# Second attention of a gated cross-attention block: the slot's projection on TensorE moved ahead of the transposes

## What is computed

```
x = x + tanh(g_xattn[0]) * attention0(layernorm(x), ctx)
x = x + tanh(g_ffn[0])   * quantised_feed_forward(layernorm(x))
x = x + tanh(g_xattn[1]) * attention1(layernorm(x), ctx, mask)
x = x + tanh(g_ffn[1])   * mixture_of_experts(layernorm(x))
```

```
q, k, v = x @ wq + bq, ctx @ wk + bk, ctx @ wv + bv      (per head)
score = q k^T / 4 * mask; where it is 0: -1e9
heads = softmax(score) v ;  out = heads @ wo + bo
```

## Time and profile before

| | |
|---|---|
| median of 3 runs | 1631.07 us (1628.36 to 1631.3) |
| the profiled execution's own time | 1624.04 us |
| its span in the trace | 1622.2 us |
| PE busy in the span | 1399.8 us (86%) |
| DVE busy | 1230.6 us (76%) |
| ACT busy | 1103.1 us (68%) |
| mean granted PE clock | 0.936 of full speed |

### The profile page before, as it was taken

One profiled execution on the slowest core, in us unless ns is written; L12 is line 12 of the kernel. 1 busy time (PEld: TensorE's weight loads), 2 busy tenths in 40 slices (PEclk: granted clock), 3 DMA queues, 4 the chain that ended last, 5 costly groups with the idle time before them and its releaser, 6 DMA issues. The chain is left out here.

```text
span 1622.2 us, 40480 instructions
## 1 busy us (share of the span) xinstructions
PE 1399.8 (86%) x15436; PEld 995.7 (61%) x15436; DVE 1230.6 (76%) x3108; ACT 1103.1 (68%) x2440; POOL 179.3 (11%) x177
## 2 busy tenths in 40 slices
PE   5899999999999993492379898989898689999996
PEld 3577666666667662340366666666666367788884
DVE  5888888888888877758778999898898877344443
ACT  5777777777777763467428889888888654366663
POOL 1000001100000002200000000000000100034443
PEclk9999999999999997797688999999999889999998
DMA  6122232332322211000011121211010072122221
GB/s 206 46 86 85 85 107 90 96 107 85 98 93 91 76 60 59 0 1 26 0 57 50 54 77 54 77 51 28 18 35 12 21 251 68 56 35 46 49 45 23
DMA packets 64924, 105.67 MB, mean 65 GB/s; under 512 B 7449, under 2 KB 38914, under 8 KB 63586
## 3 DMA queue, kind: packets, MB, share of 16 engines
q1 hardware_dynamic: 58018, 94.83, 18.6%
q0 software_dynamic: 6720, 8.27, 3.2%
HBM read 68.88 MB, written 35.11 MB: 64 GB/s over the span
## 5 line engine op out<-in xcount | busy, mean ns | idle before, releaser
L1482 ACT ACTIVATE a_p<-a_s,a_nb 112x375 f32<-112x375 f32 x256 | 140.9, 598 | 26.5 <-DVE a_nb L1585 26.2
L271 PE MATMUL a_ps_o<-a_vh,a_pt 125*128 125x64 f16 (+1 forms) x1536 | 152.8, 183 | 2.6 <-ACT a_pt L1495 0.8
L1402 PE MATMUL a_ps_t<-ident,a_p 112*128 112x112 f32 x768 | 118.1, 284 | 42.6 <-ACT a_p L1482 41.3
L273 PE MATMUL a_ps_o<-a_vh,a_pt 125*128 125x64 f16 (+1 forms) x1536 | 151.1, 182 | 0.0
L272 PE MATMUL a_ps_o<-a_vl,a_pt 125*128 125x64 f16 (+1 forms) x1536 | 151.0, 182 | 0.0
L618 ACT ACTIVATE a_p<-a_ps_s,a_nb 112x375 f32<-112x375 f32 x256 | 144.0, 573 | 2.7 <-DVE a_scaled L768 2.1
L271 PEld LDWEIGHTS a_ps_o<-a_vh,a_pt 125*128 125x128 f16 x1536 | 133.5, 98 | 14.7 <-ACT a_pt L1495 6.4
L626 ACT ACTIVATE a_pt<-a_ps_t 125x336 f16<-125x336 f32 x256 | 101.5, 448 | 59.4 <-PE a_ps_t L555 59.1
L1402 PEld LDWEIGHTS a_ps_t<-ident,a_p 112*128 112x128 f32 x768 | 79.6, 146 | 97.8 <-issue 82.7
L272 PEld LDWEIGHTS a_ps_o<-a_vl,a_pt 125*128 125x128 f16 x1536 | 130.8, 98 | 11.0 <-issue 0.2
L1585 DVE CUSTOM_DVE_ANT_0 a_s<-a_s,a_fill 112x375 f32<-112x375 f32 x256 | 130.3, 547 | 5.5
(11 more groups left out here) (443 smaller groups left out, 4486.7 us busy)
## 6 DMA issues: line engine op xcount, KB each, us to landing
a_piece<-in_w SPq DMA_DIRECT2D x72, 256.0 KB, 3.0
split_weights<-a_pair SPq DMA_DIRECT2D x72, 256.0 KB, 3.3
w<-split_weights SPq DMA_DIRECT2D x8, 1024.0 KB, 6.1
a_ctx<-in_ctxT SPq DMA_DIRECT2D x16, 375.0 KB, 3.6
ctx<-a_cx SPq DMA_DIRECT2D x16, 375.0 KB, 4.2
a_cx<-ctx SPq DMA_DIRECT2D x16, 375.0 KB, 5.9
w1h<-split_weights SPq DMA_DIRECT2D x2, 1792.0 KB, 14.8
w1l<-split_weights SPq DMA_DIRECT2D x2, 1792.0 KB, 18.0
```

The lines of the kernel that those rows point to most:

```text
L271: nc.tensor.matmul(out, wh, mh, start=(i == 0), stop=False)
L273: last = nc.tensor.matmul(out, wl, mh, start=False, stop=(i == n - 1))
L1402: mm = nc.tensor.matmul(ps_t[:, 2 * (g % 2) + i, t * S:(t + 1) * S], p32[:, g % 2, i, t * KV:t * KV + 128], ident32[0:S, 0:S], start=(t == ...
L1482: nc.scalar.activation(p32[:, g % 2, i, 0:NC], s2[:, g % 2, i, :], ACT.Exp, bias=nb[:, g % 2, i:i + 1], scale=-1.0).then_inc(exp_done, 1)
```

## The change

Within each slot of PE's loop, the slot's jobs are issued directly behind the scores, and the transposes of the pair ahead directly behind the jobs. The order of all other steps, and the order on the other engines, is as before.

```diff
@@ -1434,10 +1434,10 @@
             for g in range(SLOTS):
                 if g < G:
                     scores(g)
+                for name, b in slot_job(g):
+                    job(name, b)
                 if 0 <= g - 1 < G:
                     transposes(g - 1)
-                for name, b in slot_job(g):
-                    job(name, b)
                 if 0 <= g - 2 < G:
                     weighted_values(g - 2)
                 if 0 <= g - 1 < G:
```

## The result

The changed kernel takes 1732.89 us (median of 4 runs, 1730.77 to 1735.23), the kernel before 1629.71 beside it: ratio 1.0649, 95% interval 1.0614 to 1.0683 (the two medians divided give 1.063, inside it). That is slower by 103 us, where 1695 was forecast (64 slower) with a range up to 1730. The sign was right, the size was not, and the time lies outside the range.

A forecast was written before the change was run, and what follows sets the result against it. No engine is full; a ring of handovers bounds the second attention's pair loop. Profiled execution 1624.04 plus 60 (structure) plus 4 (clock) gives 1688; the median lies 7.0 above, so 1695 us, range 1665 to 1730.

The forecast's parts named there:

- The structural term: Second attention's pair loop: uncovered tail and job waits lengthen a batch by 4.21 or 3.64 us, 60 us in sum.
- my 3 for batch 0: Estimated growth of batch 0, which starts at half clock and lacks OT and W: 3 us.
- The tail: Slot's end, transposes' start to next scores: with no job between, ACT's copy can't be hidden; 2.07 us per slot.
- both rings: PE's pass waiting for ACT's copy (tail 2.07 us), and each job waiting for the previous job's low half.
- the wait for the low half: Slot's head: a job starts 0.83 us after its scores, not 0.58, where the previous job used both engines.
- The clock term: More PE idle in the stage means somewhat more time at half clock: +4 us, bounds 0 to +14.
- I take +4, near the first: Clock cost in the stage, near the bound of no more half-clock stretches (0): 4 us.
- twice as many stretches: Upper bound of the clock cost: the stage's later 37 us of half clock doubled, +14 us.
- The prediction's own sign of being wrong: Slots 1 and 6 still near 3.1 us, the pass not waiting, or the stage's mean clock under 0.85.
- the third rival: PE's half clock is no longer lifted for long stretches of the stage: 1765 to 1840 us, chance 0.08.
- Faster by the removed wait: The 40.6 us wait at PE's transposes goes and nothing replaces it: 1590 us, or part of that; chance 0.06.
- Only the tail is lost: Jobs find their bank free, so only slots without a wait lose: +24 to +40, 1655 to 1671 us; chance 0.15.

The follow-up runs named there:

- warm5: Changed kernel with 13 extra matmuls ahead of slot 5's job, where PE waits for Q's low half; 1676.96 us, ratio 1.0323 to the kernel before.
- pass_late: Changed kernel with PE's minus-identity pass moved from its slot's end to behind the next slot's scores; 1695.80 us, ratio 1.0438 to the kernel before.
- act_first_pass_late: Changed kernel with ACT copying the job's high half first (except Q's) and the pass behind the next slot's scores; 1633.10 us, ratio 1.0056.
- warm_all: Changed kernel with 13 extra matmuls ahead of slot 5's job and 3 ahead of the pass in seven of eight slots; 1679.16 us, ratio 1.0341.
- only5: Kernel before with only slot 5's job (V0) issued ahead of its transposes; 1626.76 us, ratio 1.0007.
- before_pass_late: Kernel before with the minus-identity pass moved behind the next slot's scores; 1621.01 us, ratio 0.9980.
- not5: Changed kernel with slot 5 undone: its job (V0) again issued behind the transposes; 1704.40 us, ratio 1.0472 to the kernel before.
- both_warm5: act_first_pass_late with 12 extra matmuls behind the pass, ahead of V0, in slot 5; 1612.35 us, ratio 0.9922 to the kernel before.
- act_first: Changed kernel with ACT copying the job's high half ahead of the transposed probabilities' high half, except in Q's slot; 1676.39 us, ratio 1.0312.

## Why the prediction missed the size

**The structural term (60 us) was right in kind and too large: about 42.** The batch without half clock is 3.63 + 3.65 + 3.60 + 3.37 + 3.16 + 5.27 + 3.76 + 3.11 = 29.55 us (slots 0 to 7; slot 5 from warm5, slot 6 from batch 9) against 26.78, +2.77 where +4.21 was forecast. Batches from 6 on: 3.51 + 3.64 + 3.60 + 3.37 + 3.16 + 5.27 + 3.76 + 2.70 = 29.01 against 26.78 − 0.32 = 26.46 (slot 0 of 3.52 for 3.84), +2.55 where +3.64 was forecast. With my 3 for batch 0, an estimate: 5 × 2.77 + 10 × 2.55 + 3 = 42 (batch 15 has no K, V or Q job and is counted like the others, as in the forecast; without it the sum is 40). Two numbers were off. The tail, from the transposes to the next scores, took 955.50 − 953.55 = 1.95 us, not 2.07: with the exponentials long done, the six transposes take 0.74, not 0.85. And a job on PE follows DVE's low half by 0.05 (956.17 to 956.22); the 0.15 of the earlier trace rows belongs to the OT job, where it is 0.15 in the changed kernel as well, and was wrongly applied to all. Together, 0.12 in eight slots and 0.10 in five of them, they account for the 1.44 us by which the batch was forecast too long.

**I found both rings but did not see that they close on each other.** The forecast treated the wait for the low half as 0.25 us added to a slot that the pass sets. pass_late showed that the ring from job to job is by itself as long as the slot: it goes through ACT's copy because the job's high half is queued behind it. That the move turns the order of PE's results against ACT's queue stood in the code, and it says how to mend it: act_first_pass_late brings the ratio from 1.0649 to 1.0056.

**The clock term failed.** The step that failed is "I take +4, near the first". 110 − 42 = 68 us of the stage's growth are left, over 228 − 52 = 176 us more at 1.2 GHz: 0.39 us for each, and the price in the forecast was 0.38. warm_all agrees: its clock of 0.91 makes 88 us at 1.2 GHz, 36 more than before, and 433.6 + 42 + 36 × 0.38 is 489 us against 489.9 measured. So the amount was wrong: the bound "twice as many stretches" stood for 37 us more, and there were 176. Between the profiled executions the forecast was 1688 and the time 1735: 18 too much for the structure hid a part of the 64 too little for the clock. And 0.38 came out right partly by luck. It was read in slot 3 alone, but the slot behind a stretch gives some back. Whole batches of the kernel before (number 7, with a stretch, and number 8, without) say 1.00 us for (1 − 0.94) / 0.5 × 27.45 = 3.3, that is 0.30:

```profile
1039.56:1067.01 27.45, 24.65 (x326) 17.10 (x326) 24.27 (x71) 23.63 (x43) 0.00 (x0) 0.94 0.21 65
1067.01:1093.46 26.45, 23.57 (x327) 16.07 (x326) 24.17 (x71) 23.49 (x43) 0.00 (x0) 1.00 0.21 67
```

The reason given for a small amount was that slot 5 idled 1.45 us at full clock. That was batch 3 of 16, and the same trace had the other case: slot 5 of batch 9, with the same idle, at 0.72 (shown with only5). Over the runs a wait of 1.35 to 1.56 us in slot 5 went with a clock of 1.00 (only5), of 0.72 to 0.77 in most batches (before_pass_late) and of 0.60 to 0.75 (not5, the changed kernel), so this row could bear no conclusion on another order. The prediction's own sign of being wrong, a mean clock under 0.85, came with 0.79. The Trainium skill's rule (TensorE: Matmul & The Clock Gate, "The HAM clock gate (the 'warmup' mystery)"), that activity lifts the half clock and idling brings it back, agrees with what warm5 and both_warm5 did (slot 5 of batch 9 from 0.75 and 0.74 to 1.00), and does not tell why the idle of only5 left it at 1.00. What came is the third rival, "the clock stays down", which had a chance of 0.08. Its lower edge took half of the stage's remaining 385 us, 73 us in time; 176 is 46% of them, and they cost 68. Its time of 1765 lies above the measured one mostly because it stood on the same structural 60 as the forecast.

**The rivals.** Faster by the removed wait: the wait was removed and nothing was gained, since PE stood at the pass and ahead of the jobs instead. Only the tail is lost: nearly right for the structure. Behind a K or a V a job started some 0.72 us after its scores (median of the batches), where a free bank gives 0.58 and the forecast had 0.83; but OT's job left PE idle for 0.78 us and V0's for 1.56. The rival's 24 to 40 us lie just under the structural 42; it had no clock in it.

**What stays open** is which pattern of work in a batch decides that the clock falls in slots 2 to 5: filling slot 5 cleared slot 5 everywhere but where the fall began earlier, filling the passes too left a stretch in slots 2 and 3 of 11 of 14 batches, act_first cleared slots 2 to 4 with slot 5 unfilled, and before_pass_late moved the fall from slot 3 to slot 5 in a kernel with no more idle time. No run separates the parts of it, nor idle time from the kind of matmul that PE does: the extra matmuls change both.

## What to carry to other kernels

When work is moved ahead on one engine, move what takes its result ahead on the next engine's queue as well; otherwise the result waits behind something that now comes later, and the two orders close a ring. A step that stands between a producer and the wait for its consumer is covering that wait, and its removal costs whatever is left uncovered, in every pass of the loop. And where many short waits appear on PE, price the clock as a second cost on top of the waits, with its range open to the upper side: here it was larger than the waits, and a few matmuls whose result nobody reads, put into the longest wait, gained 56 us in the changed kernel, 21 and 14 in two other orders, and nothing measurable in the kernel before. A row that shows full clock behind a wait is to be looked for in every pass of the loop before it is used as evidence: here one of 15 said otherwise.

## What the runs showed of the hardware

A wait of 1.5 us on PE left its clock at 1.00 in all 15 batches of one kernel (only5), in 14 of 15 of another (the kernel before, 0.72 in batch 9), and stood beside a clock of 0.60 to 0.75 in others (not5, the changed kernel), so a wait can't be judged alone. A microsecond at 1.2 GHz cost 0.30 us of a batch in the kernel before, and 0.39 of the stage's growth in the changed one. And PE busy is no sign of work: in slot 3 of batch 9 PE is busy 4.84 of 5.19 us at clock 0.50, in the same slot of batch 3 2.91 of 3.37 at 1.00.
